# An audio tower on one core: second feed-forward spread over attention's events, gates on the second layer, head sums as a tree on DVE

## The reference, cut to what matters

```python
h = conv_stack(x)
h = h + attn0(layernorm(h))      # 8 heads, softmax
h = h + ffn0(layernorm(h))       # 8 experts, the best one, with a capacity
h = h + attn1(layernorm(h))      # phases: sums over 4 heads x 5 windows, running sums over positions
h = h + ffn1(layernorm(h))       # 6 experts, the best two
```

```python
rh = relu(f @ router_w1 + router_b1)
top_w, top_i = top_k(softmax(rh @ router_w2 + router_b2), 2)
w = softmax(top_w)
h1 = relu(einsum('bsd,edh->bseh', f, expert_w1) + expert_b1)
h2 = relu(einsum('bseh,ehf->bsef', h1, expert_w2) + expert_b2)
expert_out = einsum('bsef,efo->bseo', h2, expert_w3) + expert_b3
out = sum over the two chosen experts of w * expert_out
```

## Time and profile before

| | us |
|---|---|
| Median of three runs | 1471.26 |
| Runs, from and to | 1465.64 to 1472.61 |
| The profiled execution | 1465.17 |
| Its span | 1463.1 |

### The profile page before, as it was taken

How to read it: one execution, slowest core, us unless ns; L and a number is a source line. 1 busy time by engine, 2 the same in 40 slices (tenths; PEclk the granted TensorE clock), 3 DMA queues, 4 the chain that set the end, 5 groups by cost and what they waited for, 6 DMA issues and landing times.

```text
span 1463.1 us, 26112 instructions
## 1 busy us (share of the span) xinstructions
PE 1167.1 (80%) x9805; PEld 769.0 (53%) x9805; DVE 875.2 (60%) x1807; ACT 614.5 (42%) x1249; POOL 608.9 (42%) x1193
## 2 busy tenths in 40 slices
PE   5579999999999999999999937305476674837995
PEld 3345565666666666666666623103264554734663
DVE  3434655655565565655656323146889888732998
ACT  1224555555554545545455413103352524213552
POOL 3201444734545445454554631478534635440000
PEclk9768999999999999999999967657667586666998
DMA  3100000000000000000000011211000000000000
GB/s 79 24 1 1 2 3 2 5 5 2 4 2 2 2 2 3 2 2 2 2 2 2 2 29 61 66 16 17 1 1 0 1 0 1 12 0 0 12 16 16
DMA packets 31369, 14.78 MB, mean 10 GB/s; under 512 B 27522, under 2 KB 28642, under 8 KB 31245
## 3 DMA queue, kind: packets, MB, share of 16 engines
q1 hardware_dynamic: 26637, 11.21, 3.3%
q0 software_dynamic: 4608, 1.91, 1.4%
HBM read 6.72 MB, written 7.27 MB: 10 GB/s over the span
## 4 chain that ended last, share of the span: by engine, by line
PE 63%; DVE 24%; POOL 6%; issue 4%; DMA 2%; ACT 1%; SPq 0%; POOLq 0%; DVEq 0%; ACTq 0%
PE psum L700 20%; PE psum L681 10%; PE psum L609 8%; PE psum L672 7%; PE psum L656 3%; DVE arena L1965 3%; PE psum L594 2%; DVE arena L1964 2%; DVE arena L1959 2%; PE psum L519 1%; POOL lnst L1089 1%; PE psum L614 1%; PE psum L751 1%; PE psum L764 1%; DVE lnst L1613 1%
## 5 line engine op out<-in xcount | busy, mean ns | idle before, releaser
L1355 ACT ACTIVATE arena<-psum 125x500 f32<-125x500 f32 x576 | 306.8, 585 | 342.9 <-PE psum L681 342.9
L1643 DVE TENSOR_REDUCE arena<-psum 125x1 f32<-125x500 f32 x384 | 242.6, 673 | 208.7 <-PE psum L609 208.5
L609 PE MATMUL psum<-arena 32*125 32x500 f32 (+1 forms) x1536 | 324.9, 520 | 0.6 <-ACT arena L1346 0.6
L700 PE MATMUL psum<-arena,XN 125*64 125x250 f32 x2304 | 308.6, 388 | 0.2 <-ACT arena L1355 0.2
L681 PE MATMUL psum<-arena 32*125 32x250 f32 x2304 | 293.9, 371 | 0.0
L681 PEld LDWEIGHTS psum<-arena 32*125 32x125 f32 x2304 | 216.0, 183 | 12.1 <-issue 1.4
L700 PEld LDWEIGHTS psum<-arena,XN 125*64 125x64 f32 x2304 | 140.6, 137 | 123.3 <-issue 78.0
L1646 DVE TENSOR_REDUCE arena<-psum 125x2 f32<-125x500 f32 x192 | 121.4, 674 | 72.6 <-PE psum L609 72.6
L609 PEld LDWEIGHTS psum<-arena 32*125 32x125 f32 x1536 | 128.6, 184 | 3.5 <-issue 2.1
L672 PE MATMUL psum<-arena,onesb 3*125 3x500 bf16 x576 | 123.3, 422 | 5.3 <-DMA arena<-arena 5.3
L1118 POOL TENSOR_SCALAR arena<-arena 125x4 bf16<-125x4 f32 x96 | 21.9, 229 | 217.3 <-DVE arena L1651 215.5
(11 more groups left out here) (327 smaller groups left out, 2079.0 us busy)
## 6 DMA issues: line engine op xcount, KB each, us to landing
arena<-arena SPq DMA_DIRECT2D x192, 1.5 KB
expert_in<-XN SPq DMA_DIRECT2D x8, 256.0 KB, 4.8
arena<-expert_in SPq DMA_DIRECT2D x4, 512.0 KB, 5.1
expert_out<-arena SPq DMA_DIRECT2D x4, 512.0 KB, 2.7
out<-H SPq DMA_DIRECT2D x8, 187.5 KB
expert_in<-XN,slot_in POOLq DMA_INDIRECT x48, 2.5
XN<-expert_out,slot_out POOLq DMA_INDIRECT x48, 3.9
arena<-in_L_ffn_w SPq DMA_DIRECT2D x2, 256.0 KB, 4.2
```

Of the source, the lines that this page charges most:

```text
L609: last = pe.matmul(ps[0:R, at_:at_ + hi - lo], QH[row:row + 32, b, g, j * R:(j + 1) * R], KH[row:row + 32, b, g, lo:hi], start=True, stop= ...
L700: last = pe.matmul(ctx_bank[64 * h2:64 * h2 + 64, 0:THIRD], XN[:, p, c, a, :], PR[:, x % 4, h2, i * THIRD:(i + 1) * THIRD], start=(c == 0) ...
L1355: act.activation(PR[:, x % 4, h2, :], st_bank[(2 * x + h2) % 3][0:R, 0:2 * THIRD], ACT.Exp)\
L1643: dve.reduce_max(MX[:, q % 2, 0, 2 * h2 + tile:2 * h2 + tile + 1], ps[0:R, 0:2 * THIRD], AX)\
```

## The change

It has four parts.

1. **The last feed-forward among attention's events.** `ffn_events` appends events: a head for each pair (`router`, `logit`, `gates`, one an event, from x = 6(p + 1) + 14 on) and then two steps an event. A step `(p, th, ep)` handles both sequences of the pair: two layer-1 matmuls of 64 rows (weights for one sequence no longer hold zeros for the other), two gate matmuls of 32 rows which spread the gates over the 128 hidden units of two experts, two layer-2 matmuls; ACT does four Relus; DVE multiplies the second-layer activations by the gates, straight from PSUM (`gated`). Layer 3 accumulates the bias (gates times `b3`) and three expert pairs in one PSUM bank, 12 matmuls of 64 columns for three tiles of one sequence, and DVE adds the result to `H` (`added`). Layer 1 of step k stands with layer 2 of step k - 1. After event 37 no attention is left, and what remains of heads and steps follows.
2. **The gates for one pair at a time.** The same DVE operations on 12 groups instead of 48, then a copy into a padded tile, PE transposes, ACT copies.
3. **The chunk.** POOL's part is gone. DVE forms all four products in two operations, subtracts and adds, and halves over the heads (64 of 128, then 32 of 64, for both sums at once). ACT does the scalings of key features and gated values, eight operations a chunk, with the scale from a column.
4. **The first attention.** The scores of unit 1 are formed before the loop, four of them ahead of the first shift, and the second shift moves to step 0.

The buffers of the last feed-forward now lie where pairs 1 and 2 of attention were or where the hidden layers were; POOL's memsets and the weights' DMAs come at x = 16 instead of 18. The output is stored in 16 DMAs instead of 8.

```diff
+        def ffn_events(x):
+
+            heads = 0
+            while head1 and heads < (1 if x is not None else 2):
+                kind, p = head1[0]
+                if x is not None and x <= NJ * (p + 1) + 13:
+                    break
+                events.append(head1.pop(0))
+                given.append((kind, p, x))
+                heads += 1
+            done = 0
+            while body1 and (x is None or done < PER):
+                k = body1[0][1]
+                p = steps1[min(k, len(steps1) - 1)][0]
+                now = [g for g in given if g[0:2] == ("gates", p)]
+                if x is not None and (not now or now[0][2] == x):
+                    break
+                if x is None and not now:
+                    while ("gates", p) in head1:
+                        kind, n = head1[0]
+                        events.append(head1.pop(0))
+                        given.append((kind, n, None))
+                events.append(body1.pop(0))
+                done += 1
+                if x is None and head1 and k % 2 == 1:
+                    kind, n = head1[0]
+                    events.append(head1.pop(0))
+                    given.append((kind, n, None))
...
-            return (k - 3) // 2 if k < 15 else k - 9
+            return (k - 6) // 2 if k < 12 else k - 9
 
         max_at = {}
-        for k in range(3, 3 * NQ):
+        for k in range(6, 3 * NQ):
             max_at.setdefault(max_step(k), []).append((k // 3, k % 3))
-        shift_at = {min(max_step(3 * q + 2) + 2, 3 * q - 1): q for q in range(1, NQ)}
+        shift_at = {min(max_step(3 * q + 2) + 2, 3 * q - 1) if q > 1 else 0: q for q in range(1, NQ)}
...
-        before += [("score", 0, i) for i in range(6)] + [("shift", 0)]
+        before += [("score", 0, i) for i in range(6)] + [("score", 1, i) for i in range(4)] + [("shift", 0)]
+        before += [("score", 1, i) for i in range(4, 6)]
...
+            def layer1(k):
+
+                p, th, ep = steps1[k]
+                cols = slice(p * L + th * HALF, p * L + (th + 1) * HALF)
+                for a in range(2):
+                    r = slice(64 * a, 64 * a + 64)
+                    ps, done = take(pe, ("l1", k, a))
+                    pe.matmul(ps[:, 0:HALF], e1w[r, ep, :], XT[r, cols], start=True, stop=True,
+                              tile_position=(64 * a, 0)).then_inc(done, 1)
+
+            def layer2(k):
+
+                p, th, ep = steps1[k]
+                emptied(pe, ("gt", p, th))
+                for a in range(2):
+                    r = slice(64 * a + 32 * (k % 2), 64 * a + 32 * (k % 2) + 32)
+                    ps, done = take(pe, ("gate", k, a))
+                    pe.matmul(ps[:, 0:HALF], SEL[r, ep].rearrange("r e d -> r (e d)"),
+                              GT[r, p % 2, th * HALF:(th + 1) * HALF], start=True, stop=True,
+                              tile_position=(64 * a + 32 * (k % 2), 0)).then_inc(done, 1)
+                for a in range(2):
+                    emptied(pe, ("l1", k, a))
+                    ps, done = take(pe, ("l2", k, a))
+                    pe.matmul(ps[:, 0:HALF], e2w[:, ep, :], H1[(2 * k + a) % 4], start=True, stop=True)\
+                        .then_inc(done, 1)
+
+            def layer3(n):
+
+                p, th = divmod(n, 2)
+                for a in range(2):
+                    r = slice(64 * a, 64 * a + 32)
+                    for ep in range(3):
+                        emptied(pe, ("gate", 3 * n + ep, a))
+                    ps, done = take(pe, ("l3", n, a))
+                    for m in range(3):
+                        o = ps[0:R, m * D:(m + 1) * D]
+                        pe.matmul(o, GT[r, p % 2, (3 * th + m) * R:(3 * th + m + 1) * R], b3r[r, :],
+                                  start=True, stop=False, tile_position=(64 * a, 0))
+                        for ep in range(3):
+                            last = pe.matmul(o, H2[6 * (n % 2) + 2 * ep + a][:, m * R:(m + 1) * R], e3w[:, ep, :],
+                                             start=False, stop=(ep == 2))
                     last.then_inc(done, 1)
...
-                pool.wait_ge(S["cosines"], 2 * (p + 1))
-                pool.wait_ge(S["wab"], p + 1)
-                if q:
-                    pool.wait_ge(S["uv"], q)
-                cc, sc = (x[:, g].rearrange("r g h p -> r (g h) p") for x in (TC, SC))
-                wa, wb = (over(WA[:, i, 16 * q:16 * q + 16], 16, PP) for i in range(2))
-                p2, p3 = (PT[:, i].rearrange("r g h p -> r (g h) p") for i in (2, 3))
-                pool.tensor_tensor(p2, sc, wa, ALU.mult)
-                link(pool.tensor_tensor(p3, cc, wb, ALU.mult))
-                pool.tensor_tensor(p2, p2, p3, ALU.add).then_inc(S["vsum"], 1)
-
-                pool.wait_ge(S["prod"], q + 1)
-                pool.wait_ge(S["vsum"], q + 1)
-                for i, x in ((0, TK), (1, SK)):
-                    fq = QQ[:, g, 64 + 32 * i:96 + 32 * i].rearrange("r (j a) p -> r j a p", a=2)
-                    pool.tensor_tensor(fq, x[:, tiles, 0],
-                                       over(GA[:, 5, 4 * q:4 * q + 4], 4, PP).rearrange("r (j a) p -> r j a p", a=2),
-                                       ALU.mult)
-                v = CV[:, tiles, :, 1, :].rearrange("r j a d -> r (j a) d")
...
+                act.wait_ge(S["rg"], p + 1)
+                act.wait_ge(S["gate"], p + 1)
+                for n in range(4):
+                    v = CV[:, tiles.start + n // 2, n % 2, 1, :]
+                    act.activation(v, v, ACT.Copy, scale=GA[:, 0, 4 * q + n:4 * q + n + 1])
                 act.wait_ge(S["prod"], q + 1)
-                act.wait_ge(S["vsum"], q + 1)
+                for n in range(4):
+                    key = 4 * (tiles.start + n // 2) + n % 2
+                    act.activation(QQ[:, g.start + n, 64:128].rearrange("r (i p) -> r i p", i=2), KS[:, :, key, :],
+                                   ACT.Copy, scale=GA[:, 5, 4 * q + n:4 * q + n + 1])
...
+                dve.wait_ge(S["wab"], p + 1)
+                cs = CS[:, :, 4 * g.start:4 * g.start + 16, :]
+                t4 = PT.rearrange("r i g h p -> r i (g h) p")
+                for i in range(2):
+                    w = WA[:, i:i + 2, 16 * q:16 * q + 16].unsqueeze(3).to_broadcast([R, 2, 16, PP])
+                    last = dve.tensor_tensor(t4[:, 2 * i:2 * i + 2], cs, w, ALU.mult)
+                last.then_inc(S["prod"], 1)
                 dve.wait_ge(S["prod"], q + 1)
-                link(dve.tensor_tensor(p0, p0, p1, ALU.subtract))
-                dve.reduce_sum(UV[:, 0], PT[:, 0].rearrange("r g h p -> r g p h"), AX)
-                dve.wait_ge(S["vsum"], q + 1)
-                dve.reduce_sum(UV[:, 1], PT[:, 2].rearrange("r g h p -> r g p h"), AX).then_inc(S["uv"], 1)
-                dve.wait_ge(S["uv"], q + 1)
+                dve.tensor_tensor(t4[:, 0], t4[:, 0], t4[:, 1], ALU.subtract)
+                link(dve.tensor_tensor(t4[:, 2], t4[:, 2], t4[:, 3], ALU.add))
+                h4 = PT.rearrange("r (n i) g h p -> r n i g (h p)", i=2)[:, :, 0]
+                link(dve.tensor_tensor(h4[:, :, :, 0:64], h4[:, :, :, 0:64], h4[:, :, :, 64:128], ALU.add))
+                link(dve.tensor_tensor(UV, h4[:, :, :, 0:32], h4[:, :, :, 32:64], ALU.add))
                 u, w = (UV[:, i].rearrange("r (j a) p -> r j a p", a=2) for i in (0, 1))
-                t0, t1 = (UT[:, i].rearrange("r (j a) p -> r j a p", a=2) for i in (0, 1))
+                t0, t1, t2, t3 = (UT[:, i].rearrange("r (j a) p -> r j a p", a=2) for i in range(4))
                 j = 2 * (q % 3)
                 cp, sp_ = (trig[:, i, j * PP:(j + 2) * PP].rearrange("r (j p) -> r j p", p=PP).unsqueeze(2)
                            .to_broadcast([R, 2, 2, PP]) for i in (0, 1))
-                qc, qs = (QQ[:, g, 32 * i:32 * i + 32].rearrange("r (j a) p -> r j a p", a=2) for i in (0, 1))
                 dve.tensor_tensor(t0, u, cp, ALU.mult)
-                link(dve.tensor_tensor(t1, w, sp_, ALU.mult))
-                link(dve.tensor_tensor(qc, t0, t1, ALU.subtract))
-                dve.tensor_tensor(t0, u, sp_, ALU.mult)
-                link(dve.tensor_tensor(t1, w, cp, ALU.mult))
-                dve.tensor_tensor(qs, t0, t1, ALU.add).then_inc(S["qf_ready"], 1)
+                dve.tensor_tensor(t1, w, sp_, ALU.mult)
+                dve.tensor_tensor(t2, u, sp_, ALU.mult)
+                link(dve.tensor_tensor(t3, w, cp, ALU.mult))
+                dve.tensor_tensor(QQ[:, g, 0:32], UT[:, 0], UT[:, 1], ALU.subtract)
+                dve.tensor_tensor(QQ[:, g, 32:64], UT[:, 2], UT[:, 3], ALU.add).then_inc(S["qf_ready"], 1)
...
+            def gated(k):
+
+                n, ep = divmod(k, 3)
+                if k == 0:
+                    i = jobs[("ret", 2 * NJ - 1)]
+                    dve.wait_ge(full[i % 8], i // 8 + 1)
+                for a in range(2):
+                    emptied(dve, ("l2", k, a))
```

(23 more changed lines are left out.)

381 lines of the change are left out of this document (216 added, 165 removed).

## The result

The changed kernel takes 1509.45 us (median of four runs, 1507.42 to 1512.47) against 1471.13 us before in the same comparison: ratio 1.0269, 95% interval 1.0237 to 1.0302. It is slower by 2.7%, where 1440 us was forecast and anything above 1472 was left out. The profiled execution took 1512.47 us, its span 1510.7.

What follows compares the result with a forecast made beforehand. DVE was taken as the full engine, the bound passing to PE in the new feed-forward. Attention event 23 at 1258.7 plus 175.3 us gave span 1434, execution 1436, or 1442 below the median; predicted 1440, range 1409 to 1472.

Steps and rivals of the forecast that it cites:

- head 1: Second pair's gate choice, among attention's events: 15.7 us, behind the centres of two layer norms on DVE and squares on ACT.
- Start: First attention: four scores ahead of the first shift fill PE's 3.03 us wait; -3 us, between 0 and -6.
- chunks: Attention chunks on DVE: 6.2 us each as a tree without Pool's half; -22 us, bounds -36 and -5.
- Heads: Router, logits and gates per pair: 11 us from PE's last matmul before to its next step, between 8 and 15.
- Step price: Last feed-forward on PE: layer 1, gates and layer 2 take 0.74 + 0.74 + 1.25 = 2.73 us a step.
- Third-layer price: Last feed-forward on PE: 24 matmuls of 64 columns at 0.22 us, 5.3 us after each three steps.
- Clock: Tail on PE: standstill in each head restarts it at 1.2 GHz; four returns and attention's part cost 10 us.
- rival 1: Feed-forward steps: PE does not regain 2.4 GHz, 13.5 us more per group of three; mildly 0.09, fully 0.09.
- Rival 2: Feed-forward steps: PE waits for PSUM evacuation by ACT and DVE, 0.6 us more a step, 1454 us; chance 0.13.
- Rival 3: Tail: feed-forward and heads come on top of attention's time, about 1459 us; chance 0.08 shared with another rival.

Runs made afterwards that it cites:

- p34: The kernel before with only the change's attention parts (start order, chunk trees on DVE, scalings on ACT) and the old feed-forward: 1438.97 us, ratio 0.9783.
- alt: swap1 with every other feed-forward step in the order layer 2, gates, layer 1: 1443.1 us, ratio 0.9834.
- narrow_before: The kernel before with its third-layer matmuls 64 columns wide instead of 128: 1469.76 us, ratio 0.9997.
- biasfirst2: The changed kernel with the three bias matmuls of each bank put before its nine others: 1481.15 us, ratio 1.0081.
- wide: The changed kernel with layer 3's weights and biases stored twice, so each matmul moves 128 columns instead of 64: 1476.41 us, ratio 1.0046.
- swap1: swap with one feed-forward step per attention event instead of two: 1429.47 us, ratio 0.9727.
- swapgap: swap1 with the gates' transposes two events or three steps behind the logits: 1429.0 us, ratio 0.9712.
- swaplate: swap with none of the second feed-forward among attention's events: 1460.73 us, ratio 0.9922.
- swap: The changed kernel with layer 3's weights as stationary operand, 375 activation columns moving, and three transposes a step later: 1442.86 us, ratio 0.9805.

## Why the prediction was wrong, point by point

The seven stretches behind event 23, each from landmark to landmark on PE (router, then the first step behind the gates):

| Stretch | forecast | after |
|---|---|---|
| steps 0-5 with attention's matmuls | 28.4 | 42.3 (1256.81 to 1299.14) |
| head 1 | 15.7 | 21.0 (to 1320.12) |
| steps 6-11 | 29.6 | 50.8 (to 1370.92) |
| head 2 | 14.3 | 16.3 (to 1387.24) |
| steps 12-17 | 27.7 | 49.9 (to 1437.18) |
| head 3 | 11 | 11.9 (to 1449.08) |
| the rest, DMA included | 38.6 | 61.6 (to 1510.7) |
| clock, given in one sum | 10 | in the rows above |

- **Start and chunks: right in sum.** -3 and -22 were forecast, and event 23 came 1.9 us earlier than said. The start was undersized: at the first transposes behind the first attention PE is 7.6 us earlier (852.88 us, before 860.43), beyond the bound of -6. The forecast counted one wait of 3.03 us; before, PE waited there 8.0 us in three places, for Pool and for the shifts' DMA, and now 1.4 us in one. The chunks take 87 us on DVE where 84 were forecast, meetings with Pool included. (The recorded sum for the old ones is a little low, its four first chunks add up to 55.6 us and not 55.5; nothing hangs on it.) The two parts alone gave 31 us (p34), against 25.
- **Heads: right but for head 1.** 49.2 us against 41. Of the 8.2, 5.3 are head 1, where PE waits 9.60 us for DVE behind its logits (up to 1318.68). DVE was free when the logits came (idle 2.46 us up to 1309.12), but beside Pool's work on the layer norms three of its gate operations took 1.51, 1.32 and 1.00 us in place of 0.2, so the chain took 9.5 us and not 6.3: 3.2 of the 5.3 us. The forecast had such meetings in the chunks and none in the heads.
- **Step price: mis-sized.** 3.12 us against 2.73. Each of the three forms of matmul follows another here, and 0.2 us goes at each change (alt), a term that the forecast didn't have: + 0.6. Against that a pair by itself is cheaper than its 0.74: four times 0.63 and three changes make the 3.12. 24 x 0.39 = 9 us.
- **Third-layer price: mis-sized.** 6.9 us against 5.3. 0.22 a matmul held (narrow_before, biasfirst2), but PE changes between 32 and 128 rows twelve times in a layer, which the forecast put at nothing. 8 x 1.6 = 13 us.
- **Clock: the step that failed.** Of the 78.6 us, 8 + 9 + 13 are taken; the remaining 48 come on top of the 10 that were forecast for the clock. They are rival 1, "fully", which had a chance of 0.09. The mechanism in the forecast was wrong, too: it let the clock fall only where PE stands still, in the heads. In the trace it falls in all eight third layers with PE busy all of the time. wide changes nothing on PE but the columns, and the falls there are gone: 33 us less in all, and 33 + 8 x 0.65 (its longer layers) = 38 us of clock. The other 10 or so of the 48 stay in wide, behind the heads; they are what is left over and were not measured by a run of their own.
- **Why the evidence was misread.** The 0.98 of 1279.8-1286.2 and the 0.93 of the last feed-forward were set against the clock's fall, the 0.50 of 1140-1160 for it. The first is 6.4 us long, and in the changed kernel the clock held for 3 to 6 us of narrow matmuls before it fell. The second has matmuls of 128 and 375 columns alone. The third was the only long one of these rows that is full of narrow matmuls, and it was at half clock with PE busy 19.8 of 20 us. It shows no fall (PE had stood idle for 2.91 us just before, up to 1139.66), but 20 us of such work did not bring the clock back. It was the row nearest to the new third layer and should have weighed most. The Trainium skill (TensorE: Matmul & The Clock Gate, "What's actually happening") makes the clock a matter of how busy the engine has been; here it fell with PE busy 36.20 of 36.2 us by the profile, so busy time in the profile can't stand for it. Read that way the rule would have kept 2.4 GHz in the third layers, as the forecast did, and missed the 38 us.
- **Rival 2, the evacuation loop: did not happen.** In the steps PE waits neither for ACT nor for DVE until the last one (0.82 us ahead of 1498.63). At half clock PE is so slow that this tells little, but swap1's steps at full clock show no such wait either, up to the last third layer (1.44 us). It isn't far off: in swapgap PE does wait inside steps, 3.5 us in all.
- **Rival 3, nothing overlaps: its price was right, its case was not.** It stood 19 us above the forecast; swaplate is 18 us above swap.
- **The whole, without the two mistakes:** swap removes the clock's fall and the dear third layer, and comes to 1442.86; the forecast was 1440. That agreement is partly luck, since swap's third layer is 2.1 us shorter than the forecast's 5.3 and its steps 0.39 dearer, and since the attention parts gave 31 us where 25 were forecast. The forecast overrated the new feed-forward by some 8 us all the same: swap is 4 us slower than p34, where the forecast had the feed-forward win 4.
